# The skip term D*u of a selective scan, written into the y banks by ScalarE as four scaled copies instead of by TensorE as diagonal products

## The reference, cut to what matters

```python
def step(h, inp):                     # over 1024 times
    d_t, B_t, C_t, u_t = inp
    h = h * exp(d_t[..., None] * A) + (d_t * u_t)[..., None] * B_t[:, None, :]
    y = einsum('bcn,bn->bc', h, C_t)
    return (h, y)
y = scan(...) + u * Dp                # Dp: one value per channel and layer: the skip term
y = y * silu(z)
x = x + einsum('blc,dc->bld', y, Wo)  # 8 layers, one after the other
```

## Time and profile before

| | us |
|---|---|
| median of three runs | 7812.48 (7796.15 to 7815.26) |
| span of the profiled execution | 7776.4 |
| around the span, by the median | 36.1 |
| TensorE busy | 6941.0 (89%) |
| VectorE busy | 6640.2 (85%) |
| ScalarE busy | 6441.2 (83%) |
| GpSimd busy | 5922.7 (76%) |

### The profile page before, as it was taken

One profiled execution on the slowest core, in us unless ns is written; L12 is line 12 of the kernel. 1 busy time (PEld: TensorE's weight loads), 2 busy tenths in 40 slices (PEclk: granted clock), 3 DMA queues, 4 the chain that ended last, 5 costly groups with the idle time before them and its releaser, 6 DMA issues. The chain is left out here.

```text
span 7776.4 us, 144083 instructions
## 1 busy us (share of the span) xinstructions
PE 6941.0 (89%) x40063; PEld 4774.8 (61%) x40063; DVE 6640.2 (85%) x6512; ACT 6441.2 (83%) x10314; POOL 5922.7 (76%) x4917
## 2 busy tenths in 40 slices
PE   6979999899998989999899989989999999999887
PEld 4646666666666666666666666666666666666665
DVE  3258988988898898889888988988898898889888
ACT  2258888888888888888888888888888888888887
POOL 2148887788888878788878877888888788888875
PEclk9989999999999999999999999999999999999998
DMA  4111111111111111111111111111111111111112
GB/s 161 33 43 38 40 39 46 42 38 40 42 45 43 39 37 47 42 39 40 39 47 43 40 37 42 45 43 39 39 47 43 39 39 41 45 44 38 40 38 90
DMA packets 222613, 352.40 MB, mean 45 GB/s; under 512 B 43856, under 2 KB 78448, under 8 KB 221712
## 3 DMA queue, kind: packets, MB, share of 16 engines
q1 hardware_dynamic: 218048, 332.70, 14.4%
q0 software_dynamic: 3792, 10.38, 0.4%
HBM read 325.00 MB, written 17.98 MB: 44 GB/s over the span
## 5 line engine op out<-in xcount | busy, mean ns | idle before, releaser
L875 POOL TENSOR_TENSOR drive<-du,brep 128x512 f32<-128x512 f32 x4096 | 5501.3, 1373 | 735.4 <-DVE du L1115 386.2
L907 ACT ACTIVATE ps_d<-delta,cur 128x512 f32<-128x512 f32 x4096 | 2844.0, 694 | 440.6 <-DVE state L1067 421.6
L914 ACT ACTIVATE prod<-ps_r,bcT 128x512 f32<-128x512 f32 x4096 | 2810.2, 686 | 239.0 <-PE ps_r L1221 234.4
L1221 PE MATMUL ps_r<-ident,state 128*128 128x128 f32 x16384 | 2549.8, 279 | 317.2 <-ACT prod L914 174.1
L1067 DVE TENSOR_TENSOR_SCAN state<-ps_d,carry,drive 128x512 f32<-128x512 f32 x2048 | 2504.2, 1265 | 307.5 <-PE ps_r L1221 273.0
L1067 DVE TENSOR_TENSOR_SCAN state<-ps_d,drive 128x512 f32<-128x512 f32 x2048 | 2391.5, 1208 | 299.2 <-PE ps_r L1221 235.5
L1228 PE MATMUL ps_y<-ident,prod 128*128 128x128 f32 x16384 | 2464.7, 274 | 25.9 <-ACT prod L914 25.9
L1228 PEld LDWEIGHTS ps_y<-ident,prod 128*128 128x128 f32 x16384 | 1926.5, 142 | 664.3 <-issue 514.9
L1221 PEld LDWEIGHTS ps_r<-ident,state 128*128 128x128 f32 x16384 | 1832.8, 141 | 765.7 <-ACT prod L914 493.1
L1269 PE MATMUL ps_r<-xm,w_inz_sb 128*128 128x512 f32 x1024 | 507.4, 618 | 89.6 <-ACT prod L914 89.6
L1261 PE MATMUL ps_r<-xm,w_inx_sb 128*128 128x512 f32 x1024 | 508.7, 620 | 22.1 <-ACT prod L914 14.5
(11 more groups left out here) (148 smaller groups left out, 4596.3 us busy)
## 6 DMA issues: line engine op xcount, KB each, us to landing
brep<-bc_dram SPq DMA_DIRECT2D x1024, 256.0 KB, 3.2
w_sb<-w SPq DMA_DIRECT2D x8, 1024.0 KB
w_all<-w SPq DMA_DIRECT2D x8, 1024.0 KB, 11.6
xb<-xs_dram SPq DMA_DIRECT2D x39, 128.5 KB, 2.1
w_all<-x SPq DMA_DIRECT2D x4, 1024.0 KB, 9.0
w_inx_sb<-w_in SPq DMA_DIRECT2D x8, 512.0 KB, 4.0
w_inz_sb<-w_in SPq DMA_DIRECT2D x8, 512.0 KB, 4.5
w_out_sb<-w_out SPq DMA_DIRECT2D x8, 512.0 KB, 4.0
```

Source lines behind the costliest of these rows:

```text
L875: nc.gpsimd.tensor_tensor(drive[:, k % DRIVE, :], du[:, j, :], brep[:, n % BREP, :], ALU.mult).then_inc(drive_set, 1)
L907: nc.scalar.activation(ps_d[:, k % 2, :], delta[h][:, j, :], ACT.Exp, scale=cur[h][:, a:a + 1]).then_inc(decay_set, 1)
L914: nc.scalar.activation(prod[:, t, :], ps_r[:, item_place(U, h, kind, item), :], ACT.Copy, scale=bcT[(h + 1) % 2 if item[1] == "prev" else ...
L1221: last = nc.tensor.transpose(out[:, j * P:(j + 1) * P], state[n % 2][:, j, t * P:(t + 1) * P], ident[:])
```

## The change

ScalarE gets `skip_y`: an ACTIVATE Copy from u to the y bank with D as the scale of each partition. It stands in ScalarE's slots (1,2), (1,3), (2,0), (2,0), between `exponent` and `weigh`. The waits on `gated_done` and the count `skip_set` are there, too. TensorE loses the four products, and waits in slot (2,0), ahead of its first `turn_back` of the unit, for all four copies. D is kept as one 128x32 tile, loaded once, with a column index that depends on the layer. Since the banks are no longer opened by a product with `start=True`, four products ahead of all units (`bits_set`) write each y bank once.

```diff
-GATE_AT, SKIPY_AT = [(1, 1), (1, 2), (1, 2), (1, 2)], [(1, 1), (1, 3), (1, 3), (1, 3)]
+GATE_AT, SKIPY_AT = [(1, 1), (1, 2), (1, 2), (1, 2)], [(1, 2), (1, 3), (2, 0), (2, 0)]
...
-        skip = sb("skip", [P, CB, P])
+        skip = sb("skip", [P, LAYERS * CB])
...
-            def load_skip(layer):
-                sp.dma_start(skip[:], w_skip[:, layer * CB:(layer + 1) * CB, :]).then_inc(skip_in, 16)
-
...
-            load_skip(0)
+            sp.dma_start(skip[:], w_skip).then_inc(skip_in, 16)
...
-                if U % UPL == UPL - 1 and layer + 1 < LAYERS:
-
-                    sp.wait_ge(skip_used, U + 1)
-                    load_skip(layer + 1)
...
+            def skip_y(U, kind, it, j):
+
+                if kind != "first":
+                    act.wait_ge(gated_done, CB * (U - 1) + j + 1)
+                    act.sem_inc(act_waited, 1)
+                elif j == 0:
+                    act.wait_ge(skip_in, 16)
+                    act.wait_ge(bits_set, 1)
+                    act.wait_ge(u_set, 1)
+                nc.scalar.activation(ps_y[:, j, :], u[:, j, :], ACT.Copy,
+                                     scale=skip[:, bass.ds((it // BATCH) * CB + j, 1)]).then_inc(skip_set, 1)
...
                 if not is_first(F):
-                    act.wait_ge(skip_used, F)
+                    act.wait_ge(skip_set, CB * F)
                 nc.scalar.activation(u[:], xc[:], ACT.Silu).then_inc(u_set, 1)
...
+                        for j in range(CB):
+                            if (n, t) == SKIPY_AT[j]:
+                                skip_y(U, kind, it, j)
                         if n:
                             weigh(U, h, kind, ("S", n - 1, t), U, n - 1, t)
...
-            def skip_y(U, kind, it, j):
-
-                if kind != "first":
-                    pe.wait_ge(gated_done, CB * (U - 1) + j + 1)
-                if j == 0:
-                    pe.wait_ge(skip_in, 16 * (it // BATCH) + 16)
-                    pe.wait_ge(u_set, U + 1)
-                last = nc.tensor.matmul(ps_y[:, j, :], skip[:, j, :], u[:, j, :], start=True, stop=True, skip_group_check=True)
-                if j == CB - 1:
-                    last.then_inc(skip_used, 1)
...
                         if n >= 2:
+                            if (n, t) == (2, 0):
+                                pe.wait_ge(skip_set, CB * U + CB)
                             turn_back(U, kind, ("S", n - 2, t), t)
                         if n:
                             turn_state(U, h, kind, ("S", n - 1, t), U, n - 1, t)
-                        for j in range(CB):
-                            if (n, t) == SKIPY_AT[j]:
-                                skip_y(U, kind, it, j)
...
+            for j in range(CB):
+                last = nc.tensor.matmul(ps_y[:, j, :], ident[:], xres[:, 0, 0:T], start=True, stop=True, skip_group_check=True)
+            last.then_inc(bits_set, 1)
```

More of the change, by code:

```diff
@@ L694, in mamba @@
         consts_set, cur_in, taps_in = sem("consts_set"), [sem("cur0_in"), sem("cur1_in")], [sem("taps0_in"), sem("taps1_in")]
-        skip_in, skip_used, conv_w_in = sem("skip_in"), sem("skip_used"), sem("conv_w_in")
+        skip_in, skip_set, bits_set, conv_w_in = sem("skip_in"), sem("skip_set"), sem("bits_set"), sem("conv_w_in")
+        act_waited = sem("act_waited")
         ring_ready, ring_act, ring_vec = sem("ring_ready"), sem("ring_act"), sem("ring_vec")
@@ L1503 @@
         "w_out": blocks(a["attn_W_out"].transpose(0, 2, 1), CB),
-        "w_skip": diagonals(a["attn_D_par"]),
+        "w_skip": by_layer("D_par"),
         "w_conv": diagonals(taps),
```

## The result

| | before | after |
|---|---|---|
| median, same chip | 7804.31 us | 8078.77 us |
| ratio | | 1.0368, 95% interval 1.0345 to 1.0391 |
| span of the profiled execution | 7776.4 | 8076.3 |

The change made the kernel 3.7% slower; 8055 us was forecast, 7930 to 8110 was the range.

A forecast was written before the change was run, and what follows sets the result against it. No engine was full; VectorE was taken to bind in states 0 to 3. Relief counted nothing, copies and TensorE's wait 2.15 us a unit, 3.8 with clock falls: 64 x 3.8 = 243 us on 7812.5, predicting 8055 us, range 7930 to 8110.

The forecast's parts named there:

- The relief: TensorE loses eight passes, 3.4 us a unit, 220 us in all; claimed worth nothing at the unit's end.
- The premise under it: VectorE sets the time in states 0 to 3, its rows following each other without an idle note; skip products just hidden.
- The copies' price: Each 128x512 copy on ScalarE from SBUF to PSUM takes 0.61 us, between 0.57 and 0.69 plus sequencer time.
- The wait and its queue: TensorE waits for the last copy in state 2; S(1,0), its weighing, a decay and scan (2,3) queue behind, 2.1 us later.
- The walk: ScalarE's slots from reading C3: weighing S(0,1) at 2099.47, last copy ending at 2105.53, TensorE starting 2.31 us later than before.
- The unit without the clock: Copies and TensorE's wait alone, no fall of the clock: each of 64 units 2.15 us longer.
- rival 1: The copies' chain alone, without clock falls or with falls over the idle stretch only: 7950 us; 30%.
- VectorE's wait at (2,3): A sign in the profile after: VectorE newly waits about 2 us for the decay at scan (2,3).
- The clock: TensorE's clock falls in nearly each unit behind its 4.8 us idle; two slow pairs in state 2 make units 3.8 longer.
- The term for state 6: The forecast named no cost in state 6; its added time there was nothing.
- the forecast's upper bound: Upper edge of the forecast's own case, 3.0 to 4.7 us a unit, 8005 to 8113 us; 58%.
- The 36.1 us around the span: Median less profiled span in the kernel before, added to the predicted span 8019.6 to give 8055.7.

The follow-up runs named there:

- e5_no_skip: The kernel before without the skip term: the four products and their diagonals' transfers left out, nothing in their place; ratio 1.0020 to the kernel before.
- e7: Changed kernel with copies earlier on ScalarE, and convolution block 2 moved from VectorE to TensorE in slot (1,3); 1.0156 of the kernel before.
- e10: Changed kernel with copies earlier on ScalarE, and convolution block 2 moved from VectorE to TensorE in slot (0,1); 1.0245 of the kernel before.
- e4_aside: The kernel before, products kept on TensorE, plus four scaled copies of u on ScalarE into a spare SBUF tile nobody reads; 7865.0 us, ratio 1.0126.
- e6_half_fill: The changed kernel plus two filling products on TensorE ahead of its wait for the copies; 7935.5 us, 1.0180 of the kernel before.
- e3: The changed kernel with copies earlier on ScalarE, plus one filling product on TensorE ahead of its wait; 1.0024 of the kernel before.
- e2: The changed kernel with copies earlier on ScalarE, two ahead of the reading of C3, and one gate a slot earlier; 1.0154 of the kernel before.
- e1: The changed kernel plus four filling products on TensorE ahead of its wait for the copies; 7954.0 us, 1.0247 of the kernel before.

## Why the prediction was right

**The relief is worth nothing.** Right: e5_no_skip, 1.0020. The premise under it was too strong: VectorE was said to set the time in states 0 to 3, and e7 and e10 show that TensorE is close behind it there.

**The copies' price.** 0.61 each was taken, and 0.61 is what they take (2398.62 to 2399.23, and two in 1.30), index computation and semaphore steps included. The Trainium skill, in ScalarE: Activation LUTs, section Step-by-step, has ScalarE faster to PSUM than to SBUF. Two copies of e4_aside into SBUF, in bf16, last 1.34 us where the changed kernel's two into PSUM, in fp32, last 1.30: a few hundredths in the rule's sense, with another type. It is of no use here, since the copies into SBUF start as close together, two in 2353.71 - 2352.49 = 1.22 us.

**The wait and its queue.** Right to a tenth or so. The walk had the last copy end 6.06 us after the start of the weighing of S(0,1); it is 2403.51 - 2397.44 = 6.07. TensorE's idle stretch was forecast as 4.8 and is 4.74. The unit without the clock was to be 2.15 longer; e6_half_fill has (2,0) to (3,0) 2.32 longer and (1,0) to (2,0) 0.27 shorter, 2.05 in sum. Its ratio of 1.0180 is rival 1's price, 7950 / 7812.5 = 1.0176, though partly by 19 falls in state 6 that rival 1 did not have. VectorE's wait at (2,3) was to be about 2 us and is 2.74 in the unit shown, where the clock is low.

**The clock.** Right that it falls in nearly each unit (62 of the 63 behind the first), right about two pairs at the lower clock (TensorE's four groups from 2403.57), and the unit 3.62 longer up to (3,3), 3.8 forecast. Shown by experiment: e6 differs from the changed kernel by two products ahead of the wait alone and gives back 1.9% of 3.7%, of which state 2 makes 64 x 1.73 = 111 us, 1.4%, and state 6 64 x 0.55 = 35 us, 0.4%. e3 against e2 shows the same with one product. The Trainium skill's rule on idle gaps (TensorE: Matmul & The Clock Gate, section HAM oscillation) agrees in kind. Here stretches of 4.74 and of 2.33 us stood ahead of the falls, and the second is shorter than the gaps that the page warns of.

By the sum of (2,0) to (2,3) and (2,3) to (3,0): before 5.84, e4 6.84, e6 8.16, after 9.89. Of the 4.05 in state 2, ScalarE's work is 1.0, the round trip through TensorE 1.3, the clock 1.7.

**What was missing.** The term for state 6 was nothing and is 1.04 a unit, 67 us by the traces: this is the main error of the sum, in part made up by 0.18 that was too much up to (3,3). It is why the unit came out at 117.8 us and not at the 116 to 117 that were to show it, a hair above the 4.7 of the forecast's upper bound. In the experiments the mean length of state 6 goes with the falls there: 2 falls 9.31 us, 4 falls 9.41, 12 falls 9.66, 19 falls 9.90, 22 falls 9.90, 28 falls 10.45 (e3, before, e1, e6, e4, after). The single units show that nothing else is in it. In all six, and in e2 and e5 too, a unit of half 1 without a fall takes 9.14 us on the mean, and one of half 0, where none of the 30 has a fall, 9.40. In the changed kernel 28 of the 30 units of half 1 have a fall and take 11.68 on the mean, 2.5 us more; the two in e3 take 10.57, 1.4 more.

Why one kernel has 28 and another 2 stays open. TensorE's work in state 6 is the same in all six, and its wait is mostly 1.1 to 1.3 us, shorter in e4 with 22 falls than in e3 with 2. In part the counts are those of one execution: the nine of e3 run from 7773.7 us at a mean granted clock of 0.991 to 7810.1 at 0.984, while the changed kernel's four lie within 5.4 us. There two units take 235.6 us on the mean, 234.6 to 238.4, and the falls come in half 1 one unit pair after another. That a pattern once met repeats is a guess from this, since no run set the length of the unit alone.

**Luck in the number.** The trace of after is 299.9 us longer than that of before, and 243 was added: 57 too few. The 36.1 us around the span should have been 1.7, and these 34 us too many hid more than half of the gap, so that 8055 is only 23 below 8078.8. By the medians the change costs 274.5 us, 31 more than forecast.

## What to carry to other kernels

Before moving work from one engine to another, look at what stands behind the moved piece in the new engine's order, and what the old engine must now wait for: here the last of four cheap copies set the start of a turn that three engines needed. The hole that is left on TensorE is not free either: in a loop, a wait that was work before can cost a stretch at half clock right behind it, as those of 4.74 and 2.33 us did here, and a product that nobody needs can be cheaper than the hole. Such a filling must leave room: sized to the hole at full clock, as in e1, it delays what stands behind it when the clock falls over it. A row of an engine without an idle note shows that it was never idle, not that less work on it would make the loop shorter; only taking work away shows that. And a trace shows one execution: take its time as the span and the little that the runs show around it, and set it against the median before adding to either.

## What was not expected of the hardware

The clock of TensorE fell behind a wait of 1.25 us and sixteen-row products in 28 of the units of one kernel and in 4 of another with the same work there. The two kernels differ four states earlier in the unit; what sets such falls on and off is not shown. They were worth 0.9% of this kernel's time by the traces. Where a fall lies counts as much as how many there are: e6's eight falls in state 2, over the filling alone, left (2,0) to (3,0) at 8.19 us against 8.16 without.
